# Expert choice on VectorE: all rounds behind the causal attention, or one round a step inside it

## What is computed

```python
def _L2_attn_ref(x, w_qkv, w_out):
    qkv = jnp.einsum('btd,ed->bte', x, w_qkv)
    ...
    scores = jnp.einsum('bqhd,bkhd->bhqk', q, k) * SCALE
    causal_bias = (1.0 - jnp.tril(jnp.ones((t, t), dtype=x.dtype))) * -10000.0
    attn = jax.nn.softmax(scores + causal_bias, axis=-1)
    ...
def _L2_ffn_ref(x, gate_w, w1, w2):
    ...
    probs = jax.nn.softmax(scores, axis=-1)
    g, m = jax.lax.top_k(probs.transpose(0, 2, 1), k)      # k = 128
    xin = x[batch_idx, m]
    h = jax.nn.gelu(jnp.einsum('nekd,edf->nekf', xin, w1), approximate=False)
    h = jnp.einsum('nekf,efd->nekd', h, w2)
    out = jnp.zeros((n, t, d), dtype=x.dtype).at[batch_idx, m].add(g[..., None] * h)
```

## Time and profile before

| | before |
|---|---|
| runs | 4176.8, 4176.64, 4173.5 us, median 4176.64 |
| profiled execution | span 4176.4 us, core 0 |
| PE / PEld busy | 82% / 44% |
| DVE busy | 77% |
| ACT / POOL busy | 55% / 40% |
| attention stage, first product to last | 2022.6 to 2573.8 us |
| gather, first DMA issue | 2578.8 us |

### The profile page before, as it was taken

One profiled execution on the slowest core, in us unless ns is written; L12 is line 12 of the kernel. 1 busy time (PEld: TensorE's weight loads), 2 busy tenths in 40 slices (PEclk: granted clock), 3 DMA queues, 4 the chain that ended last, 5 costly groups with the idle time before them and its releaser, 6 DMA issues. The chain is left out here.

```text
span 4176.4 us, 58564 instructions
## 1 busy us (share of the span) xinstructions
PE 3436.1 (82%) x17002; PEld 1831.7 (44%) x17002; DVE 3225.2 (77%) x5162; ACT 2286.7 (55%) x2729; POOL 1675.2 (40%) x783
## 2 busy tenths in 40 slices
PE   6847898889979978759799995699986977787775
PEld 3412333333347756635344442599975541222112
DVE  6869999999978877637687785487775768888884
ACT  4756666666622335424366663122212648989995
POOL 0008998989931100022000000000024338889986
PEclk9878999999989989968799998899998987888887
DMA  3453333333223357538423231211113452334332
GB/s 105 162 194 138 126 129 117 130 128 132 96 81 117 120 135 180 131 101 275 109 72 75 65 80 34 91 43 48 40 56 113 146 155 89 120 109 122 118 111 66
DMA packets 294113, 465.41 MB, mean 111 GB/s; under 512 B 40439, under 2 KB 237688, under 8 KB 273518
## 3 DMA queue, kind: packets, MB, share of 16 engines
q1 hardware_dynamic: 243590, 406.11, 30.0%
q10 hardware_dynamic: 50408, 57.97, 5.2%
HBM read 322.44 MB, written 141.33 MB: 111 GB/s over the span
## 5 line engine op out<-in xcount | busy, mean ns | idle before, releaser
L3314 POOL TENSOR_TENSOR distance_dist<-distance_dist,distance_least_all 128x2048 f32<-128x2048 f32 x128 | 577.0, 4537 | 113.5 <-DMA distance_least_all<-distance_least_rows 101.5
L1044 PE MATMUL mamba_psum<-mamba_hc,mamba_ident 128*128 128x512 f32 x1024 | 544.8, 643 | 86.7 <-DVE mamba_hc L947 69.9
L886 POOL TENSOR_TENSOR mamba_drive<-mamba_u,mamba_b_all 128x1024 f32<-128x1024 f32 x256 | 597.7, 2352 | 21.6 <-DMA mamba_b_all<-bc 21.6
L934 ACT ACTIVATE mamba_psum<-mamba_dt,mamba_a_neg 128x512 f32<-128x512 f32 x512 | 334.6, 683 | 288.7 <-DVE mamba_hc L947 281.6
L969 DVE TENSOR_TENSOR_SCAN mamba_psum<-mamba_psum,mamba_drive 128x512 f32<-128x512 f32 x352 | 414.9, 1215 | 43.7 <-POOL mamba_drive L886 29.4
L2355 DVE TENSOR_REDUCE causal_row_max<-causal_psum 128x1 f32<-128x512 f32 x512 | 332.7, 683 | 113.1 <-PE causal_psum L2411 103.0
L1044 PEld LDWEIGHTS mamba_psum<-mamba_hc,mamba_ident 128*128 128x128 f32 x1024 | 176.3, 195 | 410.6 <-DVE mamba_hc L947 223.5
L2314 ACT ACTIVATE causal_probs<-causal_psum 128x1024 f32<-128x1024 f32 x256 | 252.4, 1022 | 118.2 <-PE causal_psum L2434 116.0
L3407 DVE TENSOR_REDUCE distance_least<-distance_psum 128x2 f32<-128x1024 f32 x256 | 294.5, 1214 | 14.6 <-PE distance_psum L3466 14.1
L3425 DVE TENSOR_SCALAR distance_dist<-distance_psum 128x1024 f32<-128x1024 f32 x192 | 227.1, 1220 | 99.4 <-PE distance_psum L3481 93.4
L3466 PE MATMUL distance_psum<-distance_shared_k_stacks,distance_shared_q_stacks 102*128 102x512 bf16 x512 | 206.2, 499 | 118.1 <-DVE distance_least L3407 56.4
(11 more groups left out here) (455 smaller groups left out, 8228.5 us busy)
## 6 DMA issues: line engine op xcount, KB each, us to landing
mamba_b_all<-bc SPq DMA_DIRECT2D x32, 1024.0 KB
mamba_c_all<-bc SPq DMA_DIRECT2D x32, 1024.0 KB, 6.6
distance_least_all<-distance_least_rows SPq DMA_DIRECT2D x32, 1024.0 KB, 4.6
expert_weights_w<-L_ffn_w SPq DMA_DIRECT2D x16, 1024.0 KB, 4.8
z<-mamba_in_z SPq DMA_DIRECT2D x8, 1024.0 KB
xc<-mamba_in_xc SPq DMA_DIRECT2D x8, 1024.0 KB, 3.9
dt<-mamba_in_dt SPq DMA_DIRECT2D x8, 1024.0 KB, 3.9
u<-mamba_in_u SPq DMA_DIRECT2D x8, 1024.0 KB, 4.2
```

Of the source, the lines that this page charges most:

```text
L886: pool.tensor_tensor(drive[:, n % DRIVES:n % DRIVES + 2], u[:, slot, m].unsqueeze(1).broadcast_to([P, 2, T]), b_all[:, s:s + 2], ALU.mult) ...
L934: act.activation(ps[:, DECAY_BANK + n % RING], dt[:, slot, m], ACT.Exp, scale=a_neg[:, m, s:s + 1]).then_inc(decay_ready, 1)
L1044: pe.matmul(ps[:, Y_BANK + m % 2], ident[:, :], hc[:, n % PRODUCTS], start=False, stop=(s == DS - 1)).then_inc(y_summed, 1)
L3314: pool.tensor_tensor(dist[:, g % 2, kt], dist[:, g % 2, kt], least_all[:, g % 2], ALU.subtract).then_inc(shifted, 1)
```

## The change

A class `ExpertChoice` owns the tiles of the choice (`work`, `best`, `place`, the spread places, the two buffers for tokens, the first expert's weights) and lives from the start of the attention's stages to the end of the experts'. VectorE's steps are written out instead of looped (`run_unrolled`). In the steps (1,0) to (4,3), `turn` 0 to 15, it issues one round: MAX8 behind unit 8, the index search behind unit 11, the replacement behind unit 14. The cast follows at the end of step (5,0). SP issues the loads of the probabilities, of the first weights and of the tokens of batches 0 and 1 behind the first q stacks, and the writing and spreading of the places behind its last load. GpSimd makes the constants during the attention. In the gather, the loads for batches 0 and 1 and the rounds are gone. The other engines keep their loops.

```diff
+class ExpertChoice:
...
+    def load_ahead(self, sp):
+        sp.dma_start(self.work[:, :], self.probs_in).then_inc(self.probs_loaded, DMA)
+        self.load_w1(sp, 0)
+        self.load_w2(sp, 0)
+        for r in range(2):
+            self.load_xn(sp, r, r)
+
+    def spread_places(self, sp):
+        sp.wait_ge(self.found, 1)
+        sp.dma_start(self.place_dram.rearrange("b (e j) -> (b e) j", e=NE2), self.place_f[:, :]).then_inc(self.place_stored, DMA)
+        sp.wait_ge(self.place_stored, DMA)
+        for r in range(2):
+            self.load_places(sp, r, r)
...
+    def dve(self, dve, n):
+
+        k, op = divmod(n, self.OPS)
+        eight = slice(8 * k, 8 * k + 8)
+        if n == 0:
+            dve.wait_ge(self.probs_loaded, DMA)
+        else:
+            dve.wait_ge(self.top_step, n)
+        if op == 0:
+            dve.max(self.best[:, eight], self.work[:, :]).then_inc(self.top_step, 1)
+        elif op == 1:
+            dve.max_index(self.place[:, eight], self.best[:, eight], self.work[:, :]).then_inc(self.top_step, 1)
+        else:
+            dve.match_replace(self.work[:, :], self.best[:, eight], self.work[:, :], -1.0).then_inc(self.top_step, 1)
...
@@ stage_causal_attend
+        FIRST_ROUND = 4
...
                 for g in range(NG):
                     load_stack(sp, qs[:, g], q_in, 0, g, False, qk_loaded[g])
+                choice.load_ahead(sp)
                 with sp.Fori(0, NB - 1) as b:
...
                     load_next_v(b, NG - 1)
+                choice.spread_places(sp)
+
+            @block.gpsimd
+            def _(pool):
+                choice.pool(pool)
...
+                    turn = b * NG + g - FIRST_ROUND if g is not None else -1
+
...
+                    def choose(op):
+                        if 0 <= turn < ROUNDS:
+                            choice.dve(dve, turn * choice.OPS + op)
...
-                    some(range(6, UA))
+                    some(range(6, 9))
+                    choose(0)
+                    some(range(9, 12))
+                    choose(1)
+                    some(range(12, 15))
+                    choose(2)
+                    some(range(15, UA))
                     if first is not None:
                         split_maxima(*first)
+                    if turn == ROUNDS:
+                        choice.dve_found(dve)
...
-                run(dve, step)
+                run_unrolled(step)
...
@@ experts_gather
-                sp.dma_start(work[:, :], probs_in).then_inc(probs_loaded, DMA)
-                load_first(sp)
-                sp.wait_ge(found, 1)
-                sp.dma_start(place_dram.rearrange("b (e j) -> (b e) j", e=NE2), place_f[:, :]).then_inc(place_stored, DMA)
-                sp.wait_ge(place_stored, DMA)
-                with sp.Fori(0, NB // 2) as i:
+                with sp.Fori(1, NB // 2) as i:
...
-                for k in range(ROUNDS):
...
-                dve.wait_ge(top_step, 3 * ROUNDS)
-                dve.tensor_copy(place_f[:, :], place[:, :]).then_inc(found, 1)
-                dve.wait_ge(made, 2)
+                dve.wait_ge(choice.made, 2)
```

More of the change, by code:

```diff
@@ L1898 @@
 NE2 = 8
+F2 = 1024
+FT2 = F2 // P
+TOP2 = int(2.0 * T / NE2)
+ROUNDS = TOP2 // 8
+assert TOP2 == P
 CAUSAL = -1.0e4 / SCALE / NEG
@@ L1944, in make_others, with __init__, load_w1, load_w2 @@
                     [[0, 2 * GH], [-1, TT], [1, TT]], 0)
-def stage_causal(nc, w, x_in, chunks, context, gate, x_out, xn, q_parts, k_parts, v, s_out, probs):
+class ExpertChoice:
+    OPS = 3
+    def __init__(self, c, nc, w, probs_in, xn_in):
+        self.probs_in, self.xn_in, self.weights = probs_in, xn_in, w
+        self.ident = c.sb("ident", [P, P])
+        self.token = c.sb("token", [P, TT])
+        self.tokens = c.sb("tokens", [P, T])
+        self.work = c.sb("work", [NB * NE2, T])
+        self.best = c.sb("best", [NB * NE2, TOP2])
+        self.place = c.sb("place", [NB * NE2, TOP2], mybir.dt.uint32)
+        self.place_f = c.sb("place_f", [NB * NE2, TOP2])
+        self.place_all = c.sb("place_all", [P, 2, NE2 * TOP2])
+        self.xn = c.sb("xn", [P, 2, TT, D])
+        self.w1 = c.sb("w1", [P, DT, F2])
+        self.w2 = c.sb("w2", [P, FT2, D])
+        self.place_dram = nc.dram_tensor("experts_place_rows", (NB, NE2 * TOP2), F32, kind="Internal").ap()
+        self.probs_loaded, self.top_step, self.found, self.place_stored, self.ident_made, self.made = (
+            c.sem(n) for n in ("probs_loaded", "top_step", "found", "place_stored", "ident_made", "made"))
+        self.in_loaded = [c.sem(f"in_loaded{r}") for r in range(2)]
+        self.w1_loaded, self.w2_loaded = c.sem("w1_loaded"), c.sem("w2_loaded")
+    def load_w1(self, sp, e):
+        sp.dma_start(self.w1[:, :, :], self.weights["w1"][e].rearrange("(k p) f -> p k f", p=P)).then_inc(self.w1_loaded, DMA)
+    def load_w2(self, sp, e):
+        sp.dma_start(self.w2[:, :, :], self.weights["w2"][e].rearrange("(k p) d -> p k d", p=P)).then_inc(self.w2_loaded, DMA)
+    def load_xn(self, sp, b, r):
+        sp.dma_start(self.xn[:, r], token_tiles(self.xn_in, b)).then_inc(self.in_loaded[r], DMA)
+    def load_places(self, sp, b, r):
+        sp.dma_start(self.place_all[:, r], self.place_dram[b].partition_broadcast(P)).then_inc(self.in_loaded[r], DMA)
+    def load_ahead(self, sp):
[10 more added lines that the diff above has]
+            self.load_places(sp, r, r)
+    def pool(self, pool):
+        make_identity(pool, self.ident, self.ident_made)
+        pool.iota(self.token[:, :], [[P, TT]], base=0, channel_multiplier=1,
+                  allow_small_or_imprecise_dtypes=True).then_inc(self.made, 1)
+        pool.iota(self.tokens[:, :], [[1, T]], base=0, channel_multiplier=0,
+                  allow_small_or_imprecise_dtypes=True).then_inc(self.made, 1)
+    def dve(self, dve, n):
[11 more added lines that the diff above has]
+            dve.match_replace(self.work[:, :], self.best[:, eight], self.work[:, :], -1.0).then_inc(self.top_step, 1)
+    def dve_found(self, dve):
+        dve.wait_ge(self.top_step, ROUNDS * self.OPS)
+        dve.tensor_copy(self.place_f[:, :], self.place[:, :]).then_inc(self.found, 1)
@@ L1948, in stage_causal @@
+def stage_causal(nc, w, choice, x_in, chunks, context, gate, x_out, xn, q_parts, k_parts, v, s_out, probs):
     with Chip(nc, "causal_shared") as c:
@@ L2226, in _, with stage_causal_attend @@
                 batches(pe, body)
-def stage_causal_attend(nc, attention, q_in, k_in, v_in, s_out):
+def stage_causal_attend(nc, attention, choice, q_in, k_in, v_in, s_out):
     with Chip(nc, "causal") as c:
@@ L2270, in run, with run_out @@
                 step(b + 1, 1, (b + 1, 3), (b + 1, 0), (b, 3), b)
+            run_out(step)
+        def run_out(step):
             step(NB - 1, 2, None, (NB - 1, 1), (NB - 1, 0), None)
@@ L2274, in run, with run_unrolled @@
             step(None, None, None, None, (NB - 1, 3), NB - 1)
+        def run_unrolled(step):
+            step(0, 0, (0, 2), None, None, None)
+            step(0, 1, (0, 3), (0, 0), None, None)
+            for b in range(NB - 1):
+                step(b, 2, (b + 1, 0), (b, 1), (b, 0), None)
+                step(b, 3, (b + 1, 1), (b, 2), (b, 1), None)
+                step(b + 1, 0, (b + 1, 2), (b, 3), (b, 2), None)
+                step(b + 1, 1, (b + 1, 3), (b + 1, 0), (b, 3), b)
+            run_out(step)
         with nc.Block() as block:
@@ L2538, in experts_gather @@
-        ident_made, made, probs_loaded, top_step, found, place_stored = (
-            c.sem(n) for n in ("ident_made", "made", "probs_loaded", "top_step", "found", "place_stored"))
         turn_done, turn_copied = c.sem("turn_done"), c.sem("turn_copied")
-        in_loaded = [c.sem(f"in_loaded{r}") for r in range(2)]
         ready, done, copied, copy_begun = (c.sem(n) for n in ("ready", "done", "copied", "copy_begun"))
@@ L2610, in _ @@
             def _(pe):
[L2611 to L2612 removed]
+                pe.wait_ge(choice.ident_made, 2)
+                pe.wait_ge(choice.found, 1)
                 pe.transpose(ps[:, 0, 0:NB * NE2], best[:, :], ident[0:NB * NE2, 0:NB * NE2]).then_inc(turn_done, 1)
```

77 lines of the change are left out of this document (19 added, 58 removed).

## The result

The changed kernel takes 4137.1 us (median of four runs, 4134.66 to 4138.59), against 4175.07 us for the kernel before (four runs, 4169.53 to 4176.8). The ratio is 0.9909, its 95% interval 0.9894 to 0.9924: faster by 38 us, or 0.9%. The profiled execution took 4138.19 us with a span of 4136.2, 40.2 us under the span of before.

A forecast was written before the change was run, and what follows sets the result against it. VectorE's work fills TensorE's hole behind the attention, where both engines have little slack. Removing 47.4 us, adding 11.2 and saving 1.9 gives 38.1 us: 4138.5 from 4176.6, bounds 4134 to 4144, range 4130 to 4155.

The forecast's parts named there:

- The hole: TensorE's near-idle stretch between attention and gather, filled by VectorE's rounds and the wait for places; 47.4 us would be removed.
- the 0.58 from the cast to the transposes' end: Behind the barrier, VectorE's gather was taken to wait 0.58 us for TensorE's two transposes, starting at 2579.35.
- A round in a plain step: Attention step without projection: the three inserted VectorE operations would make it 0.80 us longer, in 12 of 16 steps.
- in a projection step: Attention step holding a projection: a round would cost 0.36 us, the rest hiding in idle time; 4 of 16 steps.
- The walk: One plain attention step followed, inserted operations taken as 0.60, 0.68 and 0.67 us; TensorE ends 0.80 us late.
- My upper bound of 14.5 us: Most the 16 attention rounds would cost, with operations at their gather spacing: 1.05 us a plain step, 0.48 with projection.
- By that rule the sum would be near the upper bound.: If VectorE's next operation waits for an empty pipe, the attention rounds would cost near 14.5 us instead of 11.0.
- The cast: Cast of the places behind attention step (5,0), claimed to add 0.2 us.
- The loop: Writing out VectorE's 28 looped attention steps would save 0.09 us in each of 21 plain steps, 1.9 us.
- The loads hidden: SP's five extra transfers, 3.1 MB early in the attention, share transfer engines with key stacks; counted as 0 us.
- (b): Rival: the 3.1 MB loaded early delay head group 1's attention stacks, 12 us would show, giving 4150; chance 0.04.
- (c): Rival: short TensorE waits in attention steps drop the clock to 1.2 GHz; 16 such steps give about 4360; chance 0.04.

The follow-up runs named there:

- the last three experiments: Changed kernel with rounds only in projection steps, 4129.47 us; with batch 0's tokens prepared before the barrier, 4133.66 us; with both, 4121.33 us.

## Why the prediction was right

It was 4138.5 us, and 4137.1 were measured. The terms, each against the rows:

- **The hole, 47.4 predicted, 47.6 measured.** VectorE's rounding starts 5.29 us behind the last attention product; the prediction has 5.52 (2579.35 - 2573.83). Two small misses make up the difference. VectorE waits for a signal that stands behind the transposes in TensorE's program, but TensorE's sequencer gives it without waiting for their end: the rounding starts 0.15 us after the first transpose has started and before it has ended. So the 0.58 from the cast to the transposes' end was the wrong piece. And TensorE's first instruction stands 5.14 us behind the last attention product, where I took the 4.94 of SP's first issue in the kernel before. The 4.61 us from the rounding to the first gather product are the same.
- **A round in a plain step, 0.80 predicted, 0.77 measured; in a projection step 0.36 and 0.35.** Of the plain step's the parts are right too: 0.36 for MAX8 (0.35 measured with the replacement left out), nothing for the search (shown by leaving it out), the rest for the replacement. The step in between is right as well: pair 11 starts 1.94 us behind unit 8 (2176.39 - 2174.45) where it started 1.58 behind it, so it is 0.36 late, as the walk has it. The walk with 0.60, 0.68 and 0.67 stands or falls with the overlap. My upper bound of 14.5 us was no bound, though: with the overlap forced away the rounds cost 20.1. I had lengthened the three operations to their spacing in the gather and kept the overlap of the maximum ahead of each; where neither overlaps, six neighbours in a step lose it.
- **"By that rule the sum would be near the upper bound."** VectorE: DVE Perf Modes of the Trainium skill, section "The DRAIN you can't avoid", is not borne out for these operations either, as far as the prediction quotes it: MAX8, and the value loads with which the search and the replacement begin, start before the maximum ahead of them has ended, and 10.9 us were measured. The same paragraph of the Trainium skill goes on that a next operation that is not held starts earlier, and the prediction left this out; the trace agrees with it in these earlier starts. Where waits keep the neighbours apart, the rounds cost 20.1 us, more than the bound.
- **The cast 0.2 predicted.** The step (5,0) takes 14.62 instead of 14.49, 0.13.
- **The loop, 1.9 predicted, 2.03 measured,** by itself. Net the attention was to lose 11.2 - 1.9 = 9.3 us, and the 27 steps, which hold all 16 rounds, the cast and all 21 plain steps, lost 8.84.
- **The loads hidden.** The maxima of head group 1 start 12.6 us behind those of group 0, in every kernel of this case, so (b) did not happen, and moving the weights away changed no step.
- **The clock.** It is 1.00 with 62.50 us of TensorE work in 65, and none of the 27 steps is longer than the others of its kind: (c) did not happen. TensorE: Matmul & The Clock Gate of the Trainium skill, section "A second HAM failure mode: psum-queue depth-cycling", has a kernel whose clock swings with short idle times between its groups of products; waits of 0.51 and 0.18 us in a step of 15.26 do not do this here.

By these terms the change is worth 38.8 us where 38.1 were predicted. That the time itself came within 1.4 us is in part luck: between the two profiled executions the way to the attention's first product moved by +7.2 us, and that from the first gather product to the end by -4.7 (+1.7 up to the scatter's last product, -6.3 behind it). Ahead of the attention and behind the scatter the two programs do the same work. The rows support the mechanism; a time to within 2 us they do not.

One thing the prediction did not look for: it took each step's slack as it is, and never asked where a round would be free. Its own row, 4.23 and 3.18 us of idle time in each projection step, had room for three rounds, and 10.9 us were to be had by it.

## What to carry to other kernels

Where two engines hand two buffers back and forth, the price of an operation put between is not its duration but what is left of it after the idle time at that place, so operations of 0.67 to 0.69 us cost 0, 0.35 and 0.42 us here; walk one period with the waits of both engines. Look first for the periods in which the partner does something else for some microseconds, and put long dependent chains there, in a row; in tight periods put single operations apart from each other. When serial work ahead of a barrier-bound stage is gone, look at once at what is late next (here the preparation of the first operands, then the copies of the transposes).

## What the runs showed of the hardware

**The last projection ran at either clock after the same idle time.** In the kernel before, TensorE waits 2.59 us ahead of it and its sixteen products last 5.41 us; in the changed one it waits 2.59 as well, and they last 3.72. The rows of TensorE for the changed kernel, then the windows within each of them, of before and of after:

```profile
2577.78 3.72 PE L2576 MATMUL causal_psum<-causal_shared_wo,causal_ctx 128*128 128x256 f32 x16 [2.59 <-DVE causal_ctx L326]
```
```profile
2565.00:2567.00 2.00, 2.00 (x6) 1.55 (x6) 0.00 (x0) 0.00 (x0) 0.00 (x0) 0.50 0.00 0
```
```profile
2578.00:2580.00 2.00, 2.00 (x10) 1.77 (x10) 0.00 (x0) 0.00 (x0) 0.00 (x0) 1.00 0.00 0
```

The granted clock is at the lower level, 1.2 GHz, in the one and at 2.4 GHz in the other, and that is the -1.7 us of the table. The wait ahead does not decide it by itself. Likewise the attention's third unit 0 and its fourth, between which the clock rises, lie 17.68 us apart before and 15.57 after, and 15.86, 17.66, 19.29 and 19.42 in kernels whose TensorE and VectorE do the same work there. What sets the moment stays open.

**Stages that are the same in two programs are not equally long.** The attention's first product starts at 2022.59 before, at 2029.82 after, and between 2021.8 and 2029.0 in the experiments, whose code ahead of it is that of one of the two. From the first gather product to the end it is 1545.05 before, 1540.4 after, and 1536.2 to 1547.6 in the experiments. In the stretch from 1580 to 1740 these are the windows of the changed kernel and of the kernel before:

```profile
1580.00:1740.00 160.00, 132.86 (x1880) 106.64 (x1881) 115.52 (x222) 92.55 (x135) 0.00 (x0) 0.88 0.73 174
```
```profile
1580.00:1740.00 160.00, 133.14 (x2004) 106.60 (x2005) 121.61 (x234) 97.63 (x141) 0.00 (x0) 0.93 0.75 179
```

TensorE is as long busy with fewer products done at a lower clock, 0.88 against 0.93. Of the +7.2 us, 6.4 arise here: by the same instruction of ScalarE the changed kernel is 2.4 us ahead at 1580 and 4.0 behind at 1740. The change does not set it: experiments with the changed kernel's code in this stretch reach the attention's first product as early as 2021.8. One program alone scatters as much from execution to execution: the seven times of the kernel before that were taken beside the last three experiments lie between 4164.43 and 4179.07. In which stage those executions differ is not on record. It is why an experiment with one time could not tell 5 us, and why the verdicts on those were read from step lengths.

**Waits whose counts are computed in registers may cost time.** The 0.09 us that writing the loop out takes away stand between the last maximum and the split, where two register operations work out the counts. The maxima and the split wait on computed counts throughout the loop, and all of these waits went at once, so that the two are the cause is not shown.
